# Mix product of the second attention in two row halves, a reordered feature-map attention, and the first input in two transfers

## The reference

```python
# block 5: 16 heads of 64, causal, out_w is (16, 64, 128)
a = einsum('bnst,...', q, k) * 64 ** -0.5
a = softmax(a + bias)                       # bias: cumulated, -30000 above the diagonal
mix = einsum('bnst,bntd->bnsd', a, v)
out = einsum('bnsd,ndx->bsx', mix, out_w)

# block 7: no heads; fmap(t) = elu(t) + 1
query, key, value = x @ Wq + bq, x @ Wk + bk, x @ Wv + bv
Q, K = fmap(query), fmap(key)
KV, Ksum = sum(K * value, axis=1), sum(K, axis=1)
Z = 1.0 / (Q * Ksum + 1e-06)
out = gelu((Q * KV * Z) @ Wo + bo)
```

## Time and profile before

| | us |
|---|---|
| median of three runs | 3004.04 |
| lowest and highest | 2986.36 and 3008.58 |
| the profiled execution | 3012.24 |
| its span, first to last instruction | 3010.5 |
| TensorE busy in the span | 2656.4 |
| VectorE busy | 1877.4 |
| ScalarE busy | 1768.0 |

### The profile page before, as it was taken

How to read it: one execution, slowest core, us unless ns; L and a number is a source line. 1 busy time by engine, 2 the same in 40 slices (tenths; PEclk the granted TensorE clock), 3 DMA queues, 4 the chain that set the end, 5 groups by cost and what they waited for, 6 DMA issues and landing times. The chain is left out here.

```text
span 3010.5 us, 75217 instructions
## 1 busy us (share of the span) xinstructions
PE 2656.4 (88%) x30828; PEld 1637.8 (54%) x30828; DVE 1877.4 (62%) x5214; ACT 1768.0 (59%) x3448; POOL 336.8 (11%) x710
## 2 busy tenths in 40 slices
PE   8998968888889799999998899999999999885486
PEld 3496946666666462212213556666666667563355
DVE  5699978788887562100003767788778777644752
ACT  3486846555666328999996256566656666411231
POOL 1100033222221010000000100000000000043025
PEclk9998979999999899999998999999999999897588
DMA  3220011000100202100000000000000000312003
GB/s 101 50 51 2 2 15 14 12 14 14 17 17 10 52 1 86 54 24 1 1 1 17 27 13 7 2 7 7 7 2 7 7 2 2 94 27 35 28 17 54
DMA packets 83198, 67.81 MB, mean 23 GB/s; under 512 B 40584, under 2 KB 71448, under 8 KB 82472
## 3 DMA queue, kind: packets, MB, share of 16 engines
q1 hardware_dynamic: 74408, 56.70, 7.8%
q0 software_dynamic: 8448, 6.30, 1.6%
HBM read 47.21 MB, written 19.96 MB: 22 GB/s over the span
## 5 line engine op out<-in xcount | busy, mean ns | idle before, releaser
L1717 ACT ACTIVATE arena<-ps 128x1024 f32<-128x1024 f32 x512 | 474.1, 1281 | 25.9 <-PE ps L1667 24.1
L1168 DVE CUSTOM_DVE_ANT_0 arena<-ps,arena 128x1024 f32<-128x1024 f32 (+7 forms) x384 | 349.9, 931 | 107.5 <-PE ps L1044 91.8
L2096 DVE CUSTOM_DVE_ANT_0 arena<-ps,arena 128x512 f32<-128x512 f32 (+3 forms) x640 | 373.0, 642 | 16.3 <-PE ps L1960 13.2
L1120 ACT ACTIVATE arena<-ps 128x1024 f32<-128x1024 f32 (+3 forms) x320 | 275.3, 896 | 130.9 <-PE ps L1077 127.2
L2050 ACT ACTIVATE arena<-arena 128x1152 f32<-128x1152 f32 (+15 forms) x256 | 306.0, 1200 | 60.2 <-DVE arena L2096 60.1
L1678 PE MATMUL ps<-arena 128*32 128x512 f32 x2048 | 273.0, 604 | 0.0
L1991 PE MATMUL ps<-arena 128*64 128x128 f32 x4352 | 268.8, 276 | 2.4 <-DVE arena L2111 1.5
L1960 PE MATMUL ps<-arena 64*128 64x512 f32 (+3 forms) x1280 | 266.0, 541 | 2.1 <-ACT arena L2026 1.1
L1991 PEld LDWEIGHTS ps<-arena 128*64 128x64 f32 x4352 | 234.7, 137 | 55.4 <-issue 45.7
L871 PE MATMUL ps<-arena 128*128 128x256 bf16 (+1 forms) x2176 | 238.3, 273 | 14.7 <-DVE arena L843 9.3
L1072 PE MATMUL ps<-arena 64*128 64x64 f32 x4352 | 216.4, 231 | 19.6 <-ACT arena L1120 11.8
(11 more groups left out here) (295 smaller groups left out, 4112.6 us busy)
## 6 DMA issues: line engine op xcount, KB each, us to landing
arena<-scr_q SPq DMA_DIRECT2D x256, 32.0 KB
scr_s<-scr_f SPq DMA_DIRECT2D x1, 4096.0 KB, 16.6
arena<-scr_k SPq DMA_DIRECT2D x32, 128.0 KB
arena<-by_head_k SPq DMA_DIRECT2D x16, 192.0 KB
arena<-scr_s SPq DMA_DIRECT2D x16, 192.0 KB, 2.6
arena<-by_head_q SPq DMA_DIRECT2D x28, 96.0 KB
by_head_k<-arena SPq DMA_DIRECT2D x5, 512.0 KB, 4.4
scr_x<-arena SPq DMA_DIRECT2D x2, 1024.0 KB, 5.2
```

The lines of the kernel that those rows point to most:

```text
L1120: e.activation(turned_block(u, kc), src, ACT.Exp, scale=-1.0).then_inc(exped, 1)
L1168: e.tensor_tensor_reduce(scored_block(u, g)[:, lo:hi], PS[:, 1024 * (k % 2):1024 * (k % 2) + hi - lo], NF[t][:, lo:hi], -1.0, mxs[:, col - ...
L1717: e.activation(PTR[k % RS], PS[:, at(n):at(n) + 1024], ACT.Sigmoid, scale=float(1 / np.sqrt(8.0))).then_inc(weighed, 1)
L2096: e.tensor_tensor_reduce(slot(u, t, g)[:, lo:hi], PS[:, base(step) + 512 * g:base(step) + 512 * g + hi - lo], bias, -1.0, mxs[:, col - 1:c ...
```

## The change

- **Entry**: `x` comes in two transfers, tiles 0 to 3 ahead of the constants and tiles 4 to 15 behind them. VectorE begins chunk 0 when the first has landed, and waits for the second ahead of chunk 1. ScalarE and GpSimd wait for nothing at the start. Three semaphores are merged into others.
- **Block 5**: `mix` becomes two products of 64 rows by 128 columns, one per head, in the same array shape as `score` and `turn`. `WO` needs no zeros and is loaded in one transfer. The results go into a slot of banks 0 to 5, which is held until `place` is through. `pv` waits for `keep` of unit u-2, not for `place`. The planner's cost of `mix`, its shape and the preferences change, and with them the order of the steps.
- **Block 7**: the weights are loaded when block 6 has made its last expert product (`ec["down"]` 6), the biases first. TensorE makes K and Q of chunks 0 to 2, then the last chunk's transposes, K and Q of chunk 3, and V last. ScalarE reads each bank with `relu(-(x + b))`, then takes `exp(-.)`, and also adds V's bias; VectorE reads the same bank with `max(x + b, 0)`. K's sum is made by the addition that makes K. The denominator is made ahead of the sum of K*V. Reciprocal, product, output, gelu and the addition to `X` go by chunks of 512 columns.

```diff
-        mode = {"score": 0, "turn": 0, "pv": 1, "mix": 2, "extra": 2}
+        mode = {"score": 0, "turn": 0, "pv": 1, "mix": 0, "extra": 2}
...
-                if kc or u - 2 in placed:
-                    yield "pv", max(evicted[u, kc] + 0.05, 0.0 if kc else placed[u - 2])
+                if kc or u - 2 in kept:
+                    yield "pv", max(evicted[u, kc] + 0.05, 0.0 if kc else kept[u - 2])
             if at["mix"] in kept:
-                yield "mix", kept[at["mix"]] + 0.05
+                yield "mix", max(kept[at["mix"]] + 0.05, min(free))
...
-                end = start + 0.48
+                s = take(("mix", u))
+                end = start + 0.27
...
-                placed[u] = engine("vector", end + 0.17, 0.75) + 0.1
+                free[s] = placed[u] = engine("vector", end + 0.17, 0.75) + 0.1
...
         def start_sync(e, w):
-            e.dma_start(by_tile(X), ...x...).then_inc(d_x, 16)
+            e.dma_start(by_tile(X)[:, 0:4, :], x[:, 0:4, :]).then_inc(d_x_first, 16)
             e.dma_start(CST, a["const"]).then_inc(d_const, 16)
+            e.dma_start(by_tile(X)[:, 4:NT, :], x[:, 4:NT, :]).then_inc(d_x, 16)
...
             def qkv_vector(e, w):
-                layernorm_vector(e, w, 0, hrow)
+                norm_moments(e, w, 0, 0)
+                norm_rows(e, w, 0, 0, hrow)
+                w.wait_ge(d_x, 16)
+                norm_moments(e, w, 0, 1)
+                for c in range(1, 4):
+                    if c < 3:
+                        norm_moments(e, w, 0, c + 1)
+                    norm_rows(e, w, 0, c, hrow)
...
-            plan = GroupOrder(..., {'score': 0.1, 'pv': 0.1, 'mix': 0.05, 'exp': 0.65, 'vector': 0.2})
+            plan = GroupOrder(..., {'score': 0.05, 'pv': 0.15, 'mix': -0.15, 'exp': 0.6, 'vector': 0.1, 'extra': -0.5})
...
-                for i in range(2):
-                    rows = slice(64 * i, 64 * i + 64)
-                    e.dma_start(WO[rows, i, :]..., a["s5_out"]...[rows]).then_inc(d_out, 16)
+                e.dma_start(WO.rearrange("p (g c) -> p g c", g=8), ...).then_inc(d_out, 16)
...
+                elif x[0] == "mix":
+                    w.wait_ge(placed, 2 * x[1] + 2)
...
                         if kc == 0 and u >= 2:
-                            w.wait_ge(placed, 2 * u - 2)
+                            w.wait_ge(kept, u - 1)
...
-                        e.matmul(bank(6 + u % 2, 256, 128), kept_sums(u), WO[:, :, 128 * gr:128 * gr + 128], ...).then_inc(mixed, 1)
+                        free(w, step)
+                        for g in range(2):
+                            rows = slice(64 * g, 64 * g + 64)
+                            m = e.matmul(PS[:, base(step) + 512 * g:base(step) + 512 * g + 128], kept_sums(u)[rows], WO[rows, 128 * gr:128 * gr + 128], ...)
+                        m.then_inc(mixed, 1)
...
-                for i in range(2):
-                    e.memset(WO[64 - 64 * i:128 - 64 * i, i, :], 0.0).then_inc(zeroed, 1)
...
         def stage7():
...
             def sync(e, w):
-                w.wait_ge(x_ready, 6)
+                w.wait_ge(ec["down"], 6)
...
             def tensor(e, w):
+                for i, c in front:                 # K0 K1 K2 Q0 Q1 Q2
+                    w.wait_ge(ln_ht, 24 + c + 1)
+                    product(i, c)
+                norm_turn(e, w, 6, 3, HR, 7)
+                w.wait_ge(ln_ht, 24 + 4)
+                for i, c in rest:                  # K3 Q3
+                    product(i, c)
                 for c in range(4):
+                    w.wait_ge(raised, raise_order.index((KEY, c)) + 1)
+                    w.wait_ge(taken, clip_order.index((KEY, c)) + 1)
+                    product(VALUE, c)
+                for c in range(4):
+                    w.wait_ge(normed, 2 * c + 4)
...
             def scalar(e, w):
+                    e.activation(cols(CLIPPED[i], c), bank(at[i] + c), ACT.Relu, bias=NB[:, i:i + 1], scale=-1.0).then_inc(taken, 1)
...
+                    e.activation(CLIPPED[i], CLIPPED[i], ACT.Exp, scale=-1.0).then_inc(exped, 1)
...
+                for n, (i, c) in enumerate(clip_order):   # K0..K3, Q0..Q3
+                    if n == 3:
+                        norm_take(e, w, 6, 3, 7)
+                    clip(i, c)
+                    if (i, c) == (KEY, 3):
+                        exp(KEY)
+                exp(QUERY)
+                for c in range(4):
+                    e.activation(cols(V, c), bank(c), ACT.Identity, bias=BQ[:, 2:3]).then_inc(taken, 1)
...
             def vector(e, w):
+                    e.tensor_scalar(cols(MAXED[i], c), bank(at[i] + c), BQ[:, i:i + 1], 0.0, ALU.add, ALU.max).then_inc(raised, 1)
...
+                e.tensor_scalar(M, M, -1.0, 1.0, ALU.add, ALU.add).then_inc(mapped, 1)
+                e.tensor_tensor_reduce(K, K, M, 1.0, 0.0, ALU.add, ALU.add, ks).then_inc(mapped, 1)
+                e.tensor_scalar(E, E, -1.0, 1.0, ALU.add, ALU.add).then_inc(mapped, 1)
+                e.tensor_tensor(Q, Q, E, ALU.add).then_inc(mapped, 1)
+                e.tensor_scalar(E, Q, ks, 1e-6, ALU.mult, ALU.add).then_inc(normed, 1)
+                e.tensor_tensor_reduce(M, K, V, 1.0, 0.0, ALU.mult, ALU.add, kv).then_inc(normed, 1)
...
+                for c in range(4):
+                    e.reciprocal(cols(E, c), cols(E, c)).then_inc(normed, 1)
+                    e.scalar_tensor_tensor(cols(Q, c), cols(Q, c), kv, cols(E, c), ALU.mult, ALU.mult).then_inc(normed, 1)
+                    if c >= 1:
+                        out(c - 1)
+                    if c >= 2:
+                        add(c - 2)
+                out(3)
+                add(2)
+                add(3)
```

More of the change, by code:

```diff
@@ L675, in qkv_scalar @@
             def qkv_scalar(e, w):
-                layernorm_scalar(e, w, 0)
+                norm_root(e, w, 0, 0)
+                norm_take(e, w, 0, 0, 0)
+                norm_root(e, w, 0, 1)
+                for c in range(1, 4):
+                    if c < 3:
+                        norm_root(e, w, 0, c + 1)
+                    norm_take(e, w, 0, c, c)
             def qkv_gpsimd(e, w):
@@ L1857, in extras @@
                 return [(256, True)] if u < 112 and u % 16 in (8, 10, 12, 14) else []
-            plan = GroupOrder(units, pieces, extras, 4, 12288, {'score': 0.1, 'pv': 0.1, 'mix': 0.05, 'exp': 0.65, 'vector': 0.2})
+            plan = GroupOrder(units, pieces, extras, 4, 12288, {'score': 0.05, 'pv': 0.15, 'mix': -0.15, 'exp': 0.6, 'vector': 0.1, 'extra': -0.5})
             def last_score(u):
@@ L2612, in scalar, with clip, exp @@
                 norm_root(e, w, 6, 3)
[L2613 to L2616 removed]
+                w.wait_ge(negated, 1)
+                def clip(i, c):
+                    if i == KEY:
+                        w.wait_ge(made, order.index((i, c)) + 1)
+                    else:
+                        w.wait_ge(raised, raise_order.index((i, c)) + 1)
+                    e.activation(cols(CLIPPED[i], c), bank(at[i] + c), ACT.Relu, bias=NB[:, i:i + 1], scale=-1.0).then_inc(taken, 1)
+                def exp(i):
+                    w.wait_ge(taken, max(clip_order.index((i, c)) for c in range(4)) + 1)
+                    e.activation(CLIPPED[i], CLIPPED[i], ACT.Exp, scale=-1.0).then_inc(exped, 1)
[7 more added lines that the diff above has]
+                for c in range(4):
+                    w.wait_ge(made, 8 + c + 1)
+                    e.activation(cols(V, c), bank(c), ACT.Identity, bias=BQ[:, 2:3]).then_inc(taken, 1)
                 for c in range(4):
@@ L2626, in vector @@
                 w.wait_ge(x_ready, 6)
+                w.wait_ge(d_w, 336)
+                e.tensor_scalar(NB, BQ[:, 0:2], -1.0, None, ALU.mult).then_inc(negated, 1)
                 norm_moments(e, w, 6, 3)
                 norm_rows(e, w, 6, 3, HR)
-                w.wait_ge(d_w, 336)
-                n = 0
-                for i, dst in order:
-                    for c in range(4):
-                        w.wait_ge(made, n + 1)
-                        e.tensor_scalar(cols(dst, c), bank(n % 8), BQ[:, i:i + 1], None, ALU.add).then_inc(biased, 1)
-                        n += 1
@@ L2649, in vector, with out, add @@
-                w.wait_ge(normed, 3)
-                e.reciprocal(V, V).then_inc(normed, 1)
-                w.wait_ge(normed, 4)
-                e.scalar_tensor_tensor(Q, Q, kv, V, ALU.mult, ALU.mult).then_inc(normed, 1)
-                for c in range(4):
+                def out(c):
                     w.wait_ge(mixed, c + 1)
                     e.tensor_tensor(by_four(cols(G, c)), by_four(bank(c)), BO.unsqueeze(1).to_broadcast([128, 4, 128]), ALU.add).then_inc(outed, 1)
-                for c in range(4):
+                def add(c):
```

108 lines of the change are left out of this document (51 added, 57 removed).

## The result

The changed kernel takes 2974.47 us (median of 17 runs, 2965.09 to 2992.5) against 3002.27 of the kernel before (median of 17, 2986.36 to 3010.77): a ratio of 0.9914, interval 0.9896 to 0.9931, that is 21 to 31 us less. The forecast was 2950, 52 less than that median. The direction held; half of the size is missing.

A forecast was written before the change was run, and what follows sets the result against it. TensorE was taken to bound block 5's loop, VectorE's chain block 7. Entry 3.4, block 5 36 (50 + 5 - 19) and block 7 17.4 sum to 56.8 us: 2955 from 3012.2, 2947 on the median, stated as 2950; range 2925 to 2982.

The forecast's parts named there:

- Entry: Kernel start: splitting the load of x lets VectorE begin chunk 0 earlier; gain 3.4 us, ends 0 and 3.6.
- Block 7: Block 7: earlier weights, a shorter VectorE chain and work by column chunks gain 17.4 us, ends 14 and 19.
- the middle: Block 7, from mapping K to the sum of K*V: forecast to run from 2776.7 to 2788.2.
- the tail: Block 7, from reciprocal to last additions, on VectorE: 24.7 us and some 0.6 for starts, ending at 2813.5.
- the front: Block 7's first products: twelve instructions, six taking 4.97 at the low clock and six at 0.44, ending at 2770.3.
- Block 5, the product itself: Block 5's mix: two concurrent 64-row products without a shape change save 0.41 us per unit, 128 times; taken as 50 us.
- a microsecond taken off its stream shortens the loop: Block 5's main loop: TensorE, 796 of 802 us busy, sets its length, as long as VectorE at 80% keeps up.
- Block 5, the slot: Block 5: mix's new wait for a PSUM slot costs 19 us, a third of 58; bounds 0 and 58.
- Preferences: Block 5: the planner's order changes in a way no trace shows; no separate cost, its ends those of the slot cost.
- The skill's rule: Block 5: row tiling raises PSUM pressure; by it alone the sum would be the second rival's.
- The second one: Rival, chance 0.25: block 5 gains only 8 to 12 us, total 29 to 33, about 2975.
- the signs that were named for a wrong prediction: Block 5's clock drops, VectorE passes 85% with TensorE idle, or ScalarE's PSUM reads in block 7 cost over 0.6.

The follow-up runs named there:

- the one-head kernel: Changed kernel with only the first head's mix product, into bank 6 or 7, no slot, preferences of its own: 2951.15, loop 766.5 (one run).
- the complete kernel with the halves apart: Changed kernel with both heads' products written one behind the other into bank 6 or 7, no slot, own preferences: 2978.74 against 3021.47, ratio 0.9864.
- the two other runs whose order does this: Kernel before plus a slot held by mix, fitted preferences: loop 819.6; changed kernel with one head's product, no slot, the changed kernel's preferences: loop 786.1.
- the two runs with the old preferences: Kernel before, its mix also holding a slot until place is through: loop 842.8; changed kernel with the planner's preferences of before: 3026.12, loop 865.0.
- the changed kernel on the second chip: Changed kernel, nothing altered, timed on the chip of the version with separate halves, against the kernel before: 3002.34 against 3021.47, ratio 0.9938.

## Why the prediction failed, by its own steps

**Entry: right.** Forecast 3.4, measured 3.7. First statistics at 4.08 (said: near 4), second part of `x` in at 8.66 (8.4), TensorE's transposes of chunk 1 at 11.79 (11.8), last rows' end 16.24 (16.1).

**Block 7: right.** Forecast 17.4 and a length of 52.6; measured 18.8 and 51.3. First product to last addition was forecast at 50.9 (2762.6 to 2813.5) and took 49.7. Its parts: to the end of K's exponential 13.1 (forecast 14.1), the middle to the first reciprocal 11.4 (11.5), the tail 25.2 (25.3). The one microsecond is in the front: twelve product instructions took 6.74 us to the transposes, where 4.97 and six by 0.44 had been put. In the tail, VectorE's multiplication over 512 columns took 0.75 where a quarter of 2.35 would be 0.59, and such costs were met by the 0.6 for starts. The table load was 1.28 us, with the exponential 0.02 behind it; the 2.66 of the Trainium skill (ScalarE: Activation LUTs, What ACT_TABLE_LOAD costs) does not show on this chain.

**Block 5, the product itself: the price was right, its worth was not.** A `mix` with its four instructions takes 0.32 us to the start of the next step. One behind the other, four by 0.11 would be 0.44, so the halves overlap. The changed kernel's timeline:

```profile
2213.11 0.49 PE L2015 MATMUL ps<-arena 64*128 64x128 f32 x4
...
2213.43 1.69 PE L1992 MATMUL ps<-arena 64*128 64x64 f32 x44
```

The forecast took 0.36 up to the next *shape*. Read by what stands behind the `mix`, with the old preferences: a `mix` between two scores took 0.22 us to the next step (median of 40), one between a turn and a `pv`, where the shape changes, 0.42 (median of 38). So the price was right to some 0.06 us. The load queue's waits for issue fell by 68 us, even more than the 50 that I booked. But the one-head kernel, free of the slot and with its own order, turned them into 36.7 (803.2 to 766.5), not 55: half of the missing 36 us lies here. The premise "a microsecond taken off its stream shortens the loop" was too strong, and its condition, that VectorE keeps up, was taken as met at 80% busy. A stream that is 99% busy can have VectorE close behind it; that each unit then meets VectorE's reads sooner is how I explain it, from the 57 us of waits against 37, and was not tested by itself.

**Block 5, the slot: this step failed.** I took 19 us, a third of 58, "because VectorE has slack" and because `mix` can stand anywhere. It costs up to 37 (803.1 against 766.5, with one head's product left out) and 29 in the complete kernel with the halves apart, inside the stated bounds but at their upper part. That is the other half of the missing 36. Three errors lie in it. First, I looked for the cost mainly at `mix` and asked how often *it* would wait. The waits for `place` did stay below 20 us as forecast (6.4 + 6.2, and 3.2 of TensorE itself), and it did not help: while one of three slots is held, the other two must carry all scores, turns and extras, and *their* waits for VectorE's reads of scores doubled. Secondly, slack by share is no slack by order. VectorE was 77% busy, but with the slot held each order had to choose: VectorE stands in front of the `mix` so as to free the slot at once (70.9 us here, 74.0 and 83.6 in the two other runs whose order does this), or the slot waits for VectorE (which then waits for the `mix` only 14.6 and 14.0 us, in the two runs with the old preferences, whose loops are 842.8 and 865.0). The loops with neither have 4.2 and 8.1 us of that wait. This is read from the traces of runs that differ in slot and order together; no run changes VectorE's place in the order alone. Thirdly, the hold of 3.8 us was read from one `mix`, and it was the longest of all 128 (mean 2.8); in the changed kernel it is 1.6, so the price was not in proportion to the hold. In the old shape the same slot costs only 16 us. That TensorE's slower stream hides the rest there is likely and not tested; if so, the price grows with the gain that it is to be set against.

**Preferences: not costed, and could not be.** They were noted as what no trace shows. With the old ones the changed loop is 62 us longer.

**The skill's rule.** Beside the measured slot stands TensorEngine Tiling (Array Packing) in the Trainium skill, Restrictions and Gotchas: row tiles want banks of their own and so press on PSUM. The prediction let it weigh only as far as scores waited before; the runs agree with the rule, at 29 to 37 us for this kernel.

**The rivals.** The second one gave 2975 and the time is 2974, but by another sum, and that hit is luck: block 5 gained 0 and not its 8 to 12; entry and block 7 give 22.5. Of its two mechanisms one is right (scores and other steps wait for VectorE, +45 us on the load queue) and one false (the halves do overlap). 22.5 lies in the measured interval of 21 to 31, and the same sum fits the other timed runs: block 7 and entry without block 5, 20 to 37; the changed kernel on the second chip, 9 to 28; with the halves apart, 22.5 + 29.5 = 52 in 27 to 55, at its upper end (the medians are 43 apart). That 2974 lies in the range of 2925 to 2982 owes nothing to the forecast's own sum. Of the signs that were named for a wrong prediction none came: the clock stayed at 1.00, VectorE at 77%, ScalarE's four reads of V took 2.40, 0.6 each. They watched how busy the engines are, and the loss was in the order of waits; what gave it away was the loop's length, 802 and not 766.

**Left open.** How much of the slot's price is its time and how much the order that a planner can find with it: with the same preferences the loop fell by 17 us when the slot went, with its own by 37, and no order is known to be the best. Why block 8 is 10 us or more shorter on one chip was not pursued.

## What to carry to other kernels

When an edit moves a small result from a private buffer into a shared ring, price it by the *other* users of the ring: what is the share of the ring held, for how long, how much more do they wait for their slowest reader, and what must the reader leave undone to free it in time. Take the hold from all its instances, not from one. A shape whose concurrent halves take separate banks could be had here without them, with its halves on either side of another step. And when an order written by a planner changes, compare only kernels that each have an order of their own; another kernel's preferences cost 20 to 62 us here, up to more than all the edits under test.

## What was not expected of the hardware

The granted clock in block 1's projections differs between executions of about the same work. TensorE was busy in all of each stretch shown here. The changed kernel was granted the lower of the two levels (1.2 GHz, 0.50) from about 47 to 68 us and again from 85 to 95:

```profile
46.00:56.00 10.00, 10.00 (x16) 3.77 (x16) 3.96 (x5) 2.58 (x6) 0.96 (x5) 0.57 0.82 260
56.00:66.00 10.00, 10.00 (x12) 3.42 (x13) 2.80 (x4) 2.49 (x5) 0.95 (x3) 0.50 0.83 266
...
86.00:96.00 10.00, 10.00 (x14) 3.18 (x14) 1.38 (x2) 2.33 (x5) 0.00 (x0) 0.54 0.13 52
```

The kernel before had one short dip only:

```profile
46.00:56.00 10.00, 10.00 (x21) 3.79 (x21) 6.57 (x10) 3.85 (x8) 0.86 (x3) 0.83 0.55 178
...
86.00:96.00 10.00, 10.00 (x25) 3.78 (x25) 5.49 (x6) 4.42 (x9) 1.57 (x5) 1.00 0.01 2
```

With the old entry and block 7 changed, whose code runs 2.7 ms later, it was at the low level for nearly all of these 40 us:

```profile
76.00:116.00 40.00, 40.00 (x48) 13.23 (x48) 10.32 (x12) 9.24 (x17) 2.33 (x6) 0.51 0.07 27
```

Before the search behind these projections, the low level lasted 3.4 us in the kernel before, 30.7 in the changed one and 55.8 in this last one, and the search began at 136.0, 145.4 and 159.5 us. Over all profiles it began at 132.2 to 159.5, 27 us apart, with 3.7 of that from code: as much as the whole gain of the change. It does not go with the kernel: four runs whose code is the same up to block 5 (the changed kernel again, with the old preferences, and one head with either order) began it at 145.5, 135.8, 148.3 and 132.2. Why the clock differs is open. So in this kernel a difference of one pair of profiles is first to be cleared of block 1's clock and of block 8, and then compared.
